# The second layer's preparation: three slices in work in each turn of its loop, where there were two

## The reference, cut to what matters

```python
x = x + layer0_attn(xn) + layer0_moe(xn)      # the moe rows are gathered by token
xn = (x - mean(x)) * rsqrt(var(x) + 1e-5)      # over the 256 features
h = rms(xn) * norm_w                           # input of the Mamba block
B, C, dt = h @ in_proj_w[...].T                # z and x parts are done later
dt = softplus(dt + dt_bias);  a = cumsum(-exp(A_log) * dt)   # in blocks of 128
probs = softmax(xn @ router_w);  two best of 16, weights renormalized
x = x + mamba(...) + experts(...)
```

## Time and profile before

| | us |
|---|---|
| three runs | 3400.52, 3403.2, 3411.67 (median 3403.2) |
| the profiled execution | 3401.37, its span 3399.3 |
| `front`, from its first transfer to the end of `places` | 1125.4 to 1419.4 of the span |

### The profile page before, as it was taken

One profiled execution on the slowest core, in us unless ns is written; L12 is line 12 of the kernel. 1 busy time (PEld: TensorE's weight loads), 2 busy tenths in 40 slices (PEclk: granted clock), 3 DMA queues, 4 the chain that ended last, 5 costly groups with the idle time before them and its releaser, 6 DMA issues. The chain is left out here.

```text
span 3399.3 us, 55677 instructions
## 1 busy us (share of the span) xinstructions
PE 2803.6 (82%) x16828; PEld 2069.8 (61%) x16828; DVE 2334.0 (69%) x5175; ACT 2002.7 (59%) x4381; POOL 1807.7 (53%) x1365
## 2 busy tenths in 40 slices
PE   4679999977299475468649999999999999999998
PEld 2356666656189343257537767677676767767675
DVE  3346666664356367455448888888888888888886
ACT  3334554423255344355337777777777777777776
POOL 2211111127100344233248888888888888888887
PEclk8779999989699667689769999999999999999999
DMA  4244444436633633455466656565655655556563
GB/s 137 64 129 156 151 163 158 162 137 232 152 114 124 238 119 99 104 186 179 142 192 194 182 178 188 173 192 175 209 178 173 191 176 184 183 179 186 160 195 107
DMA packets 309968, 555.61 MB, mean 163 GB/s; under 512 B 47920, under 2 KB 158768, under 8 KB 309552
## 3 DMA queue, kind: packets, MB, share of 16 engines
q1 hardware_dynamic: 295856, 514.28, 48.9%
q0 software_dynamic: 13824, 37.77, 3.5%
HBM read 435.25 MB, written 116.66 MB: 162 GB/s over the span
## 5 line engine op out<-in xcount | busy, mean ns | idle before, releaser
L2514 POOL TENSOR_TENSOR mm<-mt,cb 128x1024 f32<-128x1024 f32 x192 | 462.1, 2407 | 243.8 <-ACT mt L2473 243.8
L2456 ACT ACTIVATE mt<-a_wide,a_tok 128x128 f32<-128x128 f32 x1536 | 486.0, 388 | 13.7 <-POOL mm L2514 13.0
L2586 DVE SCALAR_TENSOR_TENSOR cv<-bank,taps,cv 128x509 f32<-128x509 f32 (+2 forms) x576 | 428.7, 744 | 13.7
L2391 PE MATMUL bank<-yz,wo 128*128 128x512 f32 x768 | 361.9, 594 | 0.0
L59 PE MATMUL bank<-f,wi 128*128 128x512 f32 x768 | 321.0, 418 | 12.0 <-DMA wi<-ssm_wi_split 12.0
L61 PE MATMUL bank<-f,wi 128*128 128x512 f32 x768 | 304.1, 396 | 0.0
L60 PE MATMUL bank<-f,wi 128*128 128x512 f32 x768 | 303.7, 395 | 0.0
L2364 PE MATMUL bank<-mm,x_tok 128*64 128x128 f32 x3072 | 210.8, 279 | 63.3 <-POOL mm L2514 44.5
L2364 PEld LDWEIGHTS bank<-mm,x_tok 128*64 128x64 f32 x3072 | 164.7, 137 | 146.7 <-POOL mm L2514 145.6
L2535 POOL TENSOR_TENSOR yz<-y,zs 128x512 f32<-128x512 f32 x192 | 245.4, 1278 | 15.1
L2531 POOL TENSOR_TENSOR y<-t 128x512 f32<-128x512 f32 x192 | 245.2, 1277 | 1.5 <-DVE t L2633 1.2
(11 more groups left out here) (446 smaller groups left out, 7506.8 us busy)
## 6 DMA issues: line engine op xcount, KB each, us to landing
wi<-ssm_wi_split SPq DMA_DIRECT2D x192, 512.0 KB, 4.2
a_wide<-a_scratch SPq DMA_DIRECT2D x192, 512.0 KB, 5.8
l_fw<-ffn_split SPq DMA_DIRECT2D x72, 768.0 KB, 4.6
ea<-ea_scratch SPq DMA_DIRECT2D x384, 128.0 KB, 3.1
wo<-ssm_wo_scaled SPq DMA_DIRECT2D x192, 128.0 KB, 3.1
ssm_wi_split<-l_s_out SPq DMA_DIRECT2D x24, 512.0 KB
sorted_scratch<-fr_zeros SPq DMA_DIRECT2D x4, 3072.0 KB
ey_x<-sorted_scratch SPq DMA_DIRECT2D x96, 128.0 KB, 2.3
```

The source lines that it names most:

```text
L2391: i = pe.matmul(bank[:, OUT + m, :], wo[:, g % R, m * P:(m + 1) * P], yz[:, g % 2], start=t == 0, stop=t == LAST)
L2456: i = act.activation(mt[:, h, chunk(j)], a_wide[:, g % R, h, chunk(j)], ACT.Relu, bias=a_tok[:, s * NJ + j, 2 * t + h:2 * t + h + 1], scal ...
L2514: pl.tensor_tensor(mm[:], mt[:], cb[:, s * NJ:(s + 1) * NJ, :].rearrange("p j t -> p (j t)") .unsqueeze(1).broadcast_to([P, 2, TS]), ALU.m ...
L2586: dve.scalar_tensor_tensor(cv[:, a:TS], bank[:, X, 0:TS - a], taps[:, t, k:k + 1], cv[:, a:TS], ALU.mult, ALU.add).then_inc(ph["tap"], 1)
```

## The change

In turn k three slices are in work. Slice a = k goes from its rows to the variance. Slice b = k - 1 is normalized: logarithms, exponentials, `xn`, `hm`, the split into `f_hi` and `f_lo`, `base`, and SP's writes of `acc` and of both parts. Slice c = k - 2 is routed, projected and stepped. There are eleven turns. `routed` and `SCATTER` move by a turn with it. `xc` of a is now written after `xn` and `hm` of b have read it, and waits for both. On PE a turn is steps(c), logits(c), rows_turned(a), tokens(c-1), project(c), mean(a), token_rows(c), turn(c), scores(c), variance(a). POOL issues the gather of a + 1 ahead of `base`. In the diff below PE's waits and the DVE's list of a turn are cut to their order; operands are as before.

```diff
-            return (k - 1) // NS - 1 if k > 1 and (k - 1) % NS == 0 else None
-        BEATS = range(G + 2)
-        SCATTER = {NS + 2: (0, 5), NS + 3: (5, 10), NS + 4: (10, NG)}
+            return (k - 2) // NS - 1 if k > 2 and (k - 2) % NS == 0 else None
+        BEATS = range(G + 3)
+        SCATTER = {NS + 3: (0, 5), NS + 4: (5, 10), NS + 5: (10, NG)}
...
 @block.sync
                     if has(a + 1):
                         fetch(a + 1)
+                    if has(b):
+                        bb, ts = at(b)
+                        done(sp, "base", b)
+                        sp.dma_start(acc_dram[bb, :, :, ts], acc[:, b % RA]).then_inc(ph[f"kept{b % RA}"], 16)
+                        done(sp, "f_lo", b)
+                        sp.dma_start(f_dram[b, 0], f_hi[:].bitcast(F32)).then_inc(ph["f_kept"], 16)
+                        sp.dma_start(f_dram[b, 1], f_lo[:].bitcast(F32)).then_inc(ph["f_kept"], 16)
                     if has(c):
                         bb, ts = at(c)
-                        done(sp, "base", c)
...
                         done(sp, "ea", c)
                         sp.dma_start(a_drams[bb][:, ts], a_log).then_inc(ph["a_out"], 16)
...
 @block.tensor
-                    done(pe, "x_tok", a - 2)
+                    done(pe, "x_tok", a - 3)
-                    done(pe, "acc_sum", min(c + 1, G - 1))
+                    done(pe, "acc_sum", min(c + 2, G - 1))
...
                         token_rows(c)
-                    if has(a):
-                        variance(a)
-                    if has(c):
                         turn(c)
                         scores(c)
+                    if has(a):
+                        variance(a)
...
 @block.scalar      # a turn's order; [x] marks the slice
-  f_hi[c]; z[a] x4; absz[c], ez[c]; rexp[c]; a_tok, w_tok[c-1]; sq[a]; b_feat, c_feat[c]; lnu[c];
-  Ln, Ln, Exp, Exp [a]; ru[c]; x_tok, b_tok, ends, ea, wend [c]
+  z[a] x4; absz[c], ez[c]; Ln, Ln [b]; lnu[c]; Exp, Exp [b]; ru, rexp [c]; a_tok, w_tok[c-1];
+  b_feat, c_feat[c]; f_hi[b]; sq[a]; x_tok, b_tok, ends, ea, wend [c]
...
 @block.gpsimd
+                    if has(a + 1):
+                        gather(a + 1)
-                    if has(c):
-                        done(pl, "xn", c)
...
+                    if has(b):
+                        done(pl, "xn", b)
+                        done(pl, "xc", b)
+                        pl.tensor_tensor(acc[:, b % RA], acc[:, b % RA], xn[:, b % 2], ALU.add).then_inc(ph["base"], 1)
...
 @block.vector      # a turn's order
-  z[a] x4; lg[c]; f_lo[c]; rmax, sh [c]; acc_sum[a]; mx, u [c]; xc[a]; d, rsum, corr, rrec, pr, max x4,
-  max_index x4, topsum, idf, toprec [c]; xn, hm x2 [a]; cr, one, sp, pick, dt, pick, adt, sh, scan, comb, rest, cb [c]
+  z[a] x4; mx, u, lg, d, rmax, corr, sh [c]; acc_sum[a]; xn, hm x2 [b]; xc[a]; cr, rsum, sp, rrec, dt, pr, adt,
+  max x4, scan, max_index x4, rest [c]; f_lo[b]; topsum, idf, toprec, one, pick, sh, pick, comb, cb [c]
+                        done(dve, "xn", a - 1)         # ahead of xc[a]
+                        done(dve, "hm", a - 1, KD)
```

More of the change, by code:

```diff
@@ L1514, in _ @@
                 for k in BEATS:
-                    a, c = k, k - 1
+                    a, b, c = k, k - 1, k - 2
                     if has(a + 1):
                         fetch(a + 1)
+                    if has(b):
[5 more added lines that the diff above has]
+                        sp.dma_start(f_dram[b, 1], f_lo[:].bitcast(F32)).then_inc(ph["f_kept"], 16)
                     if has(c):
                         bb, ts = at(c)
-                        done(sp, "base", c)
[L1521 to L1524, removed]
                         done(sp, "ea", c)
@@ L1596, in turn @@
                     done(pe, "b_tok", c - 1)
-                    if routed(c + 1) is not None:
-                        done(pe, "place", routed(c + 1), PLACE_OPS)
+                    if routed(c + 2) is not None:
+                        done(pe, "place", routed(c + 2), PLACE_OPS)
                     for j in range(NJ):
@@ L1645, in _ @@
                         token_rows(c)
+                        turn(c)
+                        scores(c)
                     if has(a):
                         variance(a)
-                    if has(c):
-                        turn(c)
-                        scores(c)
             @block.scalar
@@ L1673, in _ @@
                         act.activation(ez, absz, ACT.Exp, scale=-1.0).then_inc(ph["ez"], 1)
+                    if has(b):
+                        done(act, "var", b)
+                        done(act, "hm", b - 1, KD)
+                        done(act, "xn", b - 1)
+                        act.activation(ln[:, 0, :], bank[:, 2, :], ACT.Ln, bias=small[:], scale=1.0 + 1e-5).then_inc(ph["rr_ln"], 1)
+                        act.activation(ln[:, 1, :], bank[:, 2, :], ACT.Ln, bias=col("eps5")).then_inc(ph["ln_out"], 1)
+                    if has(c):
+                        done(act, "u", c)
+                        act.activation(lnu, u, ACT.Ln).then_inc(ph["lnu"], 1)
+                    if has(b):
+                        done(act, "ln_out", b)
+                        act.activation(ln[:, 1, :], ln[:, 1, :], ACT.Exp, scale=-0.5).then_inc(ph["rstd"], 1)
+                        done(act, "rr_ln", b)
+                        act.activation(ln[:, 0, :], ln[:, 0, :], ACT.Exp, scale=-0.5).then_inc(ph["rr"], 1)
+                    if has(c):
+                        done(act, "lnu", c)
+                        act.activation(ru, lnu, ACT.Exp, scale=-1.0).then_inc(ph["ru"], 1)
                         done(act, "shifted", c)
@@ L1681, in _ @@
                         i.then_inc(ph["tok"], 1)
+                    if has(c):
+                        done(act, "bc_ps", c)
+                        act.activation(b_feat[:], bank[:, 4, :], ACT.Copy).then_inc(ph["b_feat"], 1)
+                        act.activation(st["c_feat"][:, c * TS:(c + 1) * TS], bank[:, 5, :], ACT.Copy).then_inc(ph["c_feat"], 1)
+                    if has(b):
+                        done(act, "hm", b, KD)
+                        done(act, "bc_ps", b - 1)
+                        done(act, "f_kept", b - 1, 32)
+                        act.activation(f_hi[:], hm[:], ACT.Copy).then_inc(ph["f_hi"], 1)
                     if has(a):
@@ L1731, in _ @@
                 for k in BEATS:
-                    a, c = k, k - 1
-                    if has(c):
-                        done(pl, "xn", c)
-                        done(pl, "xc", c)
-                        pl.tensor_tensor(acc[:, c % RA], acc[:, c % RA], xn[:, c % 2], ALU.add).then_inc(ph["base"], 1)
+                    a, b = k, k - 1
                     if has(a + 1):
                         gather(a + 1)
+                    if has(b):
+                        done(pl, "xn", b)
+                        done(pl, "xc", b)
+                        pl.tensor_tensor(acc[:, b % RA], acc[:, b % RA], xn[:, b % 2], ALU.add).then_inc(ph["base"], 1)
                     if k in SCATTER:
@@ L1761, in _ @@
                     if has(c):
+                        done(dve, "dt_ps", c)
+                        done(dve, "absz", c)
+                        dve.tensor_scalar(mx, bank[0:HM, 6, :], col("dt_bias")[0:HM], 0.0, ALU.add, ALU.max).then_inc(ph["mx"], 1)
+                        done(dve, "ez", c)
+                        dve.tensor_scalar_add(u, ez, 1.0).then_inc(ph["u"], 1)
                         done(dve, "logits", c)
                         dve.tensor_copy(rt["lg"][:], bank[:, 3, 0:NJ * NE].rearrange("p (j e) -> p j e", j=NJ)).then_inc(ph["lg"], 1)
-                        done(dve, "f_hi", c)
-                        dve.tensor_tensor(f_lo[:], hm[:], f_hi[:].bitcast(F32), ALU.subtract).then_inc(ph["f_lo"], 1)
+                        done(dve, "u", c)
+                        dve.tensor_scalar_add(d, u, -1.0).then_inc(ph["d"], 1)
                         done(dve, "lg", c)
                         dve.tensor_reduce(rt["m"][:, :, 0:1], rt["lg"][:], AX.X, ALU.max).then_inc(ph["rmax"], 1)
+                        done(dve, "d", c)
+                        dve.tensor_tensor(corr, ez, d, ALU.subtract).then_inc(ph["c"], 1)
                         done(dve, "rmax", c)
@@ L1773, in _ @@
                         dve.tensor_tensor(acc[:, a % RA], bank[:, 0:KD, :], acc[:, a % RA], ALU.add).then_inc(ph["acc_sum"], 1)
[L1774 to L1779, removed]
+                    if has(b):
+                        done(dve, "rstd", b)
+                        done(dve, "base", b - 2)
+                        done(dve, "xt", b - 2)
+                        dve.tensor_tensor(xn[:, b % 2], xc[:], both(ln[:, 1, :]), ALU.mult).then_inc(ph["xn"], 1)
+                        done(dve, "rr", b)
+                        done(dve, "f_hi", b - 1)
+                        done(dve, "dt_ps", b - 1)
+                        for i in range(KD):
```

(21 more changed lines are left out.)

33 lines of the change are left out of this document (11 added, 22 removed).

## The result

| | us |
|---|---|
| changed kernel, median of 6 runs | 3386.07 (3379.72 to 3392.48) |
| kernel before, median of 6 runs | 3404.78 (3400.52 to 3411.67) |
| ratio | 0.9946, 95% interval 0.9928 to 0.9964 |
| profiled executions, before and after | 3401.37 and 3379.72 |
| section, from the start of the first `xc` to the end of the last `comb` | 254.7 before, 233.1 after |

The changed kernel is faster by 19 us; 3370 had been forecast.

What follows compares the result with a forecast made beforehand. A latency ring, not a full engine, was taken as the bound. Beats of 24.7 us (12.3 + 6.0 + 6.4), with start and end, put the last comb 33.4 us earlier: 3403.2 to about 3370 us, range 3354 to 3390.

Steps and rivals of the forecast that it cites:

- The ring that goes: DVE's xc follows hm directly, its mean already made, so PE's 16 us from steps to mean leave the ring.
- the rival with slower writes: f writes land as slowly as now, 9.4 instead of 6.0 us: beat 28.1, time 3390; chance 0.16.
- The ring that comes: Through memory: absz of slice c+1 waits for a_out of slice c; 12.3 + 6.0 + 6.4 = 24.7 us a beat.
- X: Start of xn (L1810) of a slice; X(n) is that of slice n.
- The size of `a_out`: SP's two f writes, then three small ones, up to absz: 6.0 us taken, between 3.6 and 9.4.
- a sign of being wrong: a_out landing under 4 or over 8 us after f_lo would show the forecast wrong.
- The start: acc_sum of slice 1 waits for its fetch behind 12 MB of zeros; first xn at 1167.2, third at 1214.2.
- The gather costs nothing: On POOL, moving the gather ahead of base costs nothing, since it only waits for z of the turn before.
- POOL's scatters: 22 scatters after base of slice 7 (1349), 1.27 us apart, end by 1377, before places at 1386.
- small writes that don't queue: a_out lands in 3.6 us instead of 6.0: beat 22.3, 14 us less, 3356; chance 0.12.
- Stages tied together by another wait: An in-order wait (lg for logits, f_hi for hm) keeps beats near 29 us: 3400; chance 0.06.
- The case slower than before: At ACT's wait before absz, the memory ring beats the old one; a_out at 12.6 us gives 3410; chance 0.04.

Runs made afterwards that it cites:

- the experiments on SP's queue: Changed kernel with a_out sent before SP's wait for f_lo (0.9887), between that wait and the f writes (0.9884), or with f writes sent twice (1.0007), against the kernel before.

## Why the prediction was right, and where it was off

- *The ring that goes*: right. The wait for the mean fell to 4.6 us, and the clock rose ahead of the mean as assumed: from slice 2 on it takes 1.88 to 1.90 us.
- *What came of it*: the turn was put at 24.7 us and took 25.8. 3386 lies in the range given, near its slow end; it lies outside the forecast's own range of 3362 to 3380, and the wider one holds it because it took in the rival with slower writes, which did not come as described.
- *The ring that comes*: right in every station. From X to the end of `f_lo` 12.3 were predicted and 12.3 came; from `absz` to the next X 6.4 and 6.4. The Trainium skill, "ScalarE: Activation LUTs", section "What ACT_TABLE_LOAD costs", adds a drain of 1.38 us to each table load; this trace does not show it, as 0.01 us lie between the load and the logarithm at 1237.96. That the `a_out` write takes the place of the mean was forecast, and the experiments on SP's queue show it.
- *The size of `a_out`*: the first term that was off. 6.0 us after the first f write had been taken; the six turns that count took 6.8, 6.7, 7.9, 5.7, 8.4 and 8.2, 7.3 on average and together 7.7 us more. The two last are over the 8 us that the prediction gave as a sign of being wrong; they ran beside POOL's scatters. The row that I took as nearest, an f write beside scatters alone (5.3), was no worse than what came for the f_lo write (3.6 to 5.0). But `absz` followed its landing by 0.8 to 4.4 us and not by 0.35. Part of this is that the issues on SP stretch behind the megabyte (up to 1.61 us for one small write, where it is 0.43 with `a_out` first); the rest stays open. The Trainium skill, "DMA: Bandwidth & Descriptors", section "Queues, rings and completion order", says that a semaphore increment lands only after every earlier write of its DMA engine; the doubled f writes agree with it, as they moved `absz` by 3.3 us.
- *The start*: the second. X(0) was put 14.6 us after the first `xc` and came after 22.3, 7.7 later; by X(2) 5.3 of it were left. I let the fetch land when its issue ended. In the changed kernel SP's issue of the two fetches ends at 1163.86, and `acc_sum`, which waits for the first of them, starts 6.7 us later, where 0.4 had been taken:

```profile
1151.73 12.13 SPq L1507 DMA_DIRECT2D fr_acc<-acc_scratch  x2
```
```profile
1170.55 1.23 DVE L1785 TENSOR_TENSOR fr_acc<-bank,fr_acc 128x1024 f32<-128x1024 f32 x1 [13.50 <-DMA fr_acc<-acc_scratch]
```

- *Together*: the section missed by 11.8 us. By X(2) it was 5.3, which holds 0.8 of the first `a_out`; the other five `a_out` terms add 6.9, and the rest, the turn with `places` among it (30.7 against 30.85), gives 0.4 back.
- *The gather costs nothing*: true as a cost, but undoing the move made the section 8.5 us longer, a gain that the sum took without naming it.
- *POOL's scatters*: the last 22 began after `base` of slice 7, as assumed, but took 31.4 us and not 28. They ended at 1387.2, 10 us later than forecast, and still before `places` at 1393.7.
- *Rivals*: small writes that don't queue fell (the turn is 21.4 with them ahead of the f writes, and 25.8 behind). f writes that land as slowly as before (8.3) fell, with 3.6 to 5.0. Stages tied together by another wait fell, as moving `a_out` alone moved the turn. The case slower than before was nearer than its 0.04 says: with 3.3 us more in the queue the whole gain is gone.

## What to carry to other kernels

When a loop is cut into more stages, look for tiles that go to memory and are written again in the next turn: their write can become the ring, at the latency of the queue that it stands in. A small write on which a ring waits belongs ahead of the large ones on its queue, or its data in a tile that is dead until later. That alone was worth nothing while another ring was longer (0.9994), and more than the stages themselves once it was not (38 us of the section against 21.6). Price such a write from its issue to the waiter, issue slots included, not from the landing of the transfer ahead of it. And follow a gain to the end of the function: 10 us of one section's gain were gone by the end of `places`.

## What the runs showed of the hardware

- Issues on SP took longer behind large transfers: 0.43 to 0.47 us for the last `a_out` write in the kernel before, up to 1.61 behind the megabyte of f writes in the changed one, and 12.1 us for the two fetches behind the zeros in the changed kernel.
- PE's clock: with the mean at the full clock in the same turn (1.88 us), the variance ran at it too after PE had idled 1.53 us (with `ea` in `adt`, the fetch first and the variance early) and 2.40 us (with `ea` in `adt`), in 1.98 us each; after 2.95 and 3.05 us (with `ea` in `adt` and the fetch first) it ran at the half clock, in 3.78.
- `hm` is two instructions of one shape. In the kernel before they take from 0.74 to 2.83 us each; POOL's `base` starts with them, as the prediction has it. No run moved `base` away from them, so its part in this is not shown.
- The kernel before takes 3405 us on one chip and 3455 to 3460 on three others (a single run on the third), 1.5 to 1.6% apart.
